# AdaLN attention and mixture-of-experts block: two-part modulation load, and another order of the prologue's products

## The reference

```python
mod = (silu(c) @ wmod).reshape(8, 6, 1, 128)
sa, ca, ga, sb, cb, gb = mod[:, 0], ..., mod[:, 5]   # gates ga, gb: size at least 0.25
h = layernorm(x) * (1 + ca) + sa
q, k, v = einsum('bsx,xAnh->Abnsh', h, w);  q = q + q_bias
a = q @ k.T * 64 ** -0.5 + relative_causal(q @ emb.T)
#   emb = sinusoids @ positional
x = x + ga * (softmax(masked(a)) @ v @ out_kernel + out_bias)
h = layernorm(x) * (1 + cb) + sb
x = x + gb * moe(h)        # 16 experts, capacity 256, one expert a token
```

## Time and profile before

| | us |
|---|---|
| median of 3 runs | 893.81 (893.18 to 894.71) |
| the profiled execution | 891.26 |
| its span, first to last instruction | 889.4 |
| PE busy / ACT busy / DVE busy in it | 865.1 / 710.7 / 667.8 |
| mean granted clock of PE | 0.992 |

### The profile page before, as it was taken

The page is one execution under the profiler, slowest core; times in us unless marked ns, Lnnn a source line. Parts: engine busy times, 40 slices in busy tenths (PEclk is TensorE's granted clock), DMA queues, the critical chain, the costliest instruction groups (busy, mean ns, idle before and its releaser), DMA issues.

```text
span 889.4 us, 17673 instructions
## 1 busy us (share of the span) xinstructions
PE 865.1 (97%) x5607; PEld 689.4 (78%) x5607; DVE 667.8 (75%) x2059; ACT 710.7 (80%) x1978; POOL 532.5 (60%) x796
## 2 busy tenths in 40 slices
PE   7999999999999999999999999999999999999994
PEld 6777777777777887777877777877777887777894
DVE  4778777786779677777879677877778677865794
ACT  4888889888888888888888889888888888873441
POOL 2655555666656765666566755676657646663454
PEclk8999999999999999999999999999999999999998
DMA  7000790000000100000000000000000000005960
GB/s 286 4 1 1 204 247 14 13 19 18 13 14 1 37 1 13 13 19 18 14 13 1 27 13 13 1 21 2 13 13 12 11 13 13 3 28 180 299 210 22
DMA packets 25053, 41.29 MB, mean 46 GB/s; under 512 B 3286, under 2 KB 17095, under 8 KB 24576
## 3 DMA queue, kind: packets, MB, share of 16 engines
q1 hardware_dynamic: 21600, 33.86, 12.7%
q0 software_dynamic: 3072, 5.94, 1.9%
q10 hardware_dynamic: 288, 0.36, 0.1%
HBM read 25.80 MB, written 16.82 MB: 48 GB/s over the span
## 4 chain that ended last, share of the span: by engine, by line
PE 82%; POOL 4%; issue 3%; DVE 1%; ACT 1%; DMA 1%; POOLq 0%; DVEq 0%; ACTq 0%
PE bank L858 22%; PE bank L823 16%; PE bank L888 16%; PE bank L868 15%; PE bank L895 5%; PE bank L844 4%; POOL out L510 3%; PE bank L855 3%; ACT prob L617 0%; POOL prob L455 0%; DMA x<-xbuf 0%; PE bank L903 0%; PE bank L808 0%; PE bank L1048 0%; PE bank L924 0%
## 5 line engine op out<-in xcount | busy, mean ns | idle before, releaser
L455 POOL TENSOR_SCALAR prob<-prob,rsum 128x128 f32<-128x128 f32 (+3 forms) x512 | 263.9, 534 | 221.8 <-DVE rsum L1233 216.1
L617 ACT ACTIVATE prob<-srow,nmax 128x512 f32<-128x512 f32 (+3 forms) x512 | 286.6, 561 | 65.7 <-DVE nmax L1221 62.5
L1221 DVE CUSTOM_DVE_ANT_0 srow<-bank,consts 128x512 f32<-128x512 f32 (+3 forms) x512 | 247.0, 488 | 88.2 <-issue 66.9
L868 PE MATMUL bank<-consts,prob 128*128 128x128 f32 x1280 | 201.9, 272 | 0.2 <-POOL prob L455 0.2
L868 PEld LDWEIGHTS bank<-consts,prob 128*128 128x128 f32 x1280 | 158.3, 141 | 22.7 <-issue 0.6
L448 POOL TENSOR_TENSOR qlo<-qx,qhi 128x384 fp32r<-128x384 f32 x128 | 129.1, 1009 | 49.5 <-ACT qhi L582 48.2
L626 ACT ACTIVATE pt<-bank 128x384 f32<-128x384 f32 x318 | 152.0, 495 | 1.4 <-PE bank L868 1.3
L888 PE MATMUL bank<-pt,v 128*64 128x512 f32 (+3 forms) x1024 | 152.0, 439 | 0.3 <-issue 0.2
L858 PE MATMUL bank<-khi,qhi 128*128 128x512 f32 (+2 forms) x384 | 145.7, 379 | 3.1 <-DVE nmax L1221 1.9
L1238 DVE SCALAR_TENSOR_TENSOR qx<-bank,qbias,consts 128x512 f32<-128x512 f32 x128 | 94.2, 736 | 60.2 <-PE bank L823 60.1
L858 PE MATMUL bank<-khi,qlo 128*128 128x512 f32 (+2 forms) x384 | 130.0, 339 | 0.0
(11 more groups left out here) (194 smaller groups left out, 1420.1 us busy)
## 6 DMA issues: line engine op xcount, KB each, us to landing
xbuf<-fill SPq DMA_DIRECT2D x4, 1540.0 KB, 23.2
x<-xbuf SPq DMA_DIRECT2D x14, 385.0 KB
raw<-in_w SPq DMA_DIRECT2D x16, 256.0 KB
prob<-in_w SPq DMA_DIRECT2D x16, 256.0 KB
h2T<-in_xt SPq DMA_DIRECT2D x8, 256.0 KB, 2.7
out<-row SPq DMA_DIRECT2D x8, 256.0 KB, 2.3
x<-in_x SPq DMA_DIRECT2D x1, 1792.0 KB, 13.3
modb<-mod_rows SPq DMA_DIRECT2D x1, 1536.0 KB, 7.3
```

The lines of the kernel that those rows point to most:

```text
L455: end = gp.tensor_scalar(part, part, rsum[:, par, 4 * h + q:4 * h + q + 1], 1.0, ALU.mult, ALU.mult)
L617: act.activation(prob[:, par, h, QOFF[q]:QOFF[q] + P * (q + 1)], srow[:, k % 4, 0:P * (q + 1)], ACT.Exp, bias=nmax[:, par, k:k + 1], scale ...
L868: last = pe.transpose(out[:, n * P:(n + 1) * P], prob[:, par, h, QOFF[q] + k * P:QOFF[q] + (k + 1) * P], ident)
L1221: dve.tensor_tensor_reduce(out=srow[:, k % 4, 0:w], in0=scb[k % 2][:, 0:w], in1=mask[:, S - w:S], scale=-1.0, scalar=BIG, op0=ALU.add, op1 ...
```

## The change

Six things are edited; the rest of the kernel is the same.

- `wmod` is loaded in two parts, sections 0 and 1 (128 KB) and 2 to 5 (256 KB), from ACT's queue behind its two loads, where it was one load on SP's queue, fifth there.
- Only the products of sections 0 and 1 stand ahead of the transposes. Those of 3, 4 and 2 follow them, into another PSUM bank, behind a wait for the second load.
- DVE copies the first two to `modT` ahead of `low_g(0, 1)`, and the three others behind `low(0)` (vlo). Later readers wait for `modT` 3, and TensorE too in round 2 of the first step, ahead of writing that bank.
- `w_table(1, 4)` moves from before the query products to behind the key product; `high_g` and `low_g` of pairs 1 to 3 move behind the key's evacuation on ACT and DVE.
- On ACT the cast of V's weights (`high_wv`) moves ahead of `high_q(0, 0)`.
- Fillers: 30 become 20, 16 become 8, the 8 behind `w_table(1, 4)` go, 16 become 6.

```diff
--- before.py
+++ after.py
@@ -258,7 +258,6 @@
             sp.dma_start(smallT[:, :], cols_d).then_inc(s["small"], 16)
             sp.dma_start(ident, consts_d[:, 0:128]).then_inc(s["ident"], 16)
             sp.dma_start(h2T[HD:P, :], ktab_d).then_inc(s["ktab"], 16)
-            sp.dma_start(wmod[:, :, :], wmod_d.rearrange("p (a b) -> p a b", a=6)).then_inc(s["wmod"], 16)
             sp.dma_start(consts[:, 512:], consts_d[:, 128:]).then_inc(s["consts"], 16)
             for h in range(2):
                 sp.dma_start(kx[HD:P, h, :], ktab_d[:, 0:P]).then_inc(s["kxt"], 16)
@@ -523,6 +522,9 @@
 
             act.dma_start(x[:, 2:QT, :], x_d[:, 2:QT, :]).then_inc(s["x0"], 16)
             act.dma_start(wall[:, 0:1, :], wall_d[:, 0:1, :]).then_inc(s["wall0"], 16)
+            wmod_v = wmod_d.rearrange("p (a b) -> p a b", a=6)
+            act.dma_start(wmod[:, 0:2, :], wmod_v[:, 0:2, :]).then_inc(s["wmod"], 16)
+            act.dma_start(wmod[:, 2:6, :], wmod_v[:, 2:6, :]).then_inc(s["wmodb"], 16)
 
             def high_g(a0, a1, after, name):
 
@@ -718,11 +720,11 @@
             high_wq(1, 4, 0)
             high_wq(1, 4, 1)
             high_wk(1, 4)
-            high_g(1, 4, 3, "whi")
+            high_wv()
             high_q(0, 0)
-            high_wv()
             evac_k(0, 0)
             evac_k(0, 1)
+            high_g(1, 4, 3, "whi")
             batches(turn)
             def high_w1(r, landed):
 
@@ -795,11 +797,15 @@
 
             pe.wait_ge(s["silu"], 1)
             pe.wait_ge(s["wmod"], 16)
-            for i, m in enumerate((0, 3, 1, 4, 2)):
-                last = pe.matmul(bank[0][:, i * B:(i + 1) * B], wmod[:, m, :], silu[:, 3, :], start=True, stop=True)
-            last.then_inc(s["mod_mm"], 1)
+            def mod_table(out, *sections):
+
+                for i, m in enumerate(sections):
+                    last = pe.matmul(out[:, i * B:(i + 1) * B], wmod[:, m, :], silu[:, 3, :], start=True, stop=True)
+                last.then_inc(s["mod_mm"], 1)
+
+            mod_table(bank[0], 0, 1)
             pe.wait_ge(s["ident"], 16)
-            idle(30)
+            idle(20)
 
             def turn_x(n, out=xtb):
 
@@ -809,9 +815,11 @@
                 last.then_inc(s["t_x"], 1)
 
             turn_x(0, opb)
+            pe.wait_ge(s["wmodb"], 16)
+            mod_table(trb[1], 3, 4, 2)
             pe.matmul(otb[0:B, 0:3 * D], silu[:, 3, :], wmod[:, 3:6, :].rearrange("p a d -> p (a d)"),
                       start=True, stop=True).then_inc(s["mod_mm"], 1)
-            idle(16)
+            idle(8)
 
             def project(out, a, cols, n, name):
 
@@ -956,6 +964,7 @@
             def first_step(k):
 
                 if k == 2:
+                    pe.wait_ge(s["modT"], 3)
                     w_table(4, PAIRS)
                 if k == 4:
                     pe.wait_ge(s["wv"], 2)
@@ -1028,18 +1037,17 @@
                         pe.wait_ge(s["wgc"], 2)
                     project_q(j + 1, n, m, 1, 8 * B if last and V_OF[a][0] else j + 4 if before else 2)
 
-            pe.wait_ge(s["wall1"], 16)
-            w_table(1, 4)
-            idle(8)
             pe.wait_ge(s["fhi"], 3)
             pe.wait_ge(s["flo"], 3)
             project_q(0, None, 0, 0)
             project_q(0, None, 0, 1)
             project_k(0, None, 0)
+            pe.wait_ge(s["wall1"], 16)
+            w_table(1, 4)
             pe.wait_ge(s["wall2"], 16)
             b_table(1, PAIRS)
             pe.wait_ge(s["hn"], 1)
-            idle(16, opb)
+            idle(6, opb)
             pe.wait_ge(s["kxt"], 32)
             pe.wait_ge(s["kt"], 4)
             def fill_in(n):
@@ -1195,13 +1203,10 @@
             dve.tensor_tensor(wlo[:, 0, 2 * P:3 * P], wall[:, 0, P:2 * P], whi[:, 0, 2 * P:3 * P], ALU.subtract)\
                 .then_inc(s["flo"], 1)
             xhat1(0)
+            dve.wait_ge(s["mod_mm"], 1)
+            dve.tensor_copy(modT[:, 0, :], bank[0][:, 0:B]).then_inc(s["modT"], 1)
+            dve.tensor_scalar(modT[:, 1, :], bank[0][:, B:2 * B], 1.0, None, ALU.add).then_inc(s["modT"], 1)
             low_g(0, 1, "fhi", 3, "flo")
-
-            dve.wait_ge(s["mod_mm"], 1)
-            half = lambda c: bank[0][:, c * B:(c + 2) * B].rearrange("p (i b) -> p i b", i=2)
-            dve.tensor_copy(modT[:, 0:3:2, :], half(0)).then_inc(s["modT"], 1)
-            link(dve.tensor_copy(modT[:, 4, :], bank[0][:, 4 * B:5 * B]))
-            dve.tensor_scalar(modT[:, 1:4:2, :], half(2), 1.0, None, ALU.add).then_inc(s["modT"], 1)
 
             def low_table():
 
@@ -1211,6 +1216,10 @@
 
             low_table()
             low(0)
+            dve.wait_ge(s["mod_mm"], 2)
+            link(dve.tensor_copy(modT[:, 2, :], trb[1][:, 0:B]))
+            link(dve.tensor_scalar(modT[:, 3, :], trb[1][:, B:2 * B], 1.0, None, ALU.add))
+            dve.tensor_copy(modT[:, 4, :], trb[1][:, 2 * B:3 * B]).then_inc(s["modT"], 1)
 
             def scores(j, par, k):
 
@@ -1362,7 +1371,7 @@
 
                 spread = lambda t: t.rearrange("p (b e) -> p b e", e=E)
                 if i == 0:
-                    dve.wait_ge(s["modT"], 2)
+                    dve.wait_ge(s["modT"], 3)
                     dve.memset(ones32, 1.0).then_inc(s["scr"], 1)
                     dve.memset(wgc[:, :, E:2 * E], 0.0).then_inc(s["scr"], 1)
                     for half, m in ((0, 3), (1, 2)):
@@ -1495,16 +1504,16 @@
             def rows_of():
 
                 dve.wait_ge(s["misc"], 48)
-                dve.wait_ge(s["mod_mm"], 2)
+                dve.wait_ge(s["mod_mm"], 3)
                 dve.tensor_copy(mrow[:, :, :].rearrange("p a d -> p (a d)"), otb[0:B, 0:3 * D]).then_inc(s["mev"], 1)
 
             dve.wait_ge(s["consts"], 16)
             dve.wait_ge(s["open"], 1)
             dve.wait_ge(s["bias"], 2)
-            low_g(1, 4, "whi", 4, "wlo")
             evac_q(0, 0, 0)
             evac_q(0, 0, 1)
             low_k(0, 0)
+            low_g(1, 4, "whi", 4, "wlo")
             batches(turn)
             def low_w1(e, par):
                 slot = e % 8
```

More of the change, by code:

```diff
@@ L185, in program @@
         mod_dram = nc.dram_tensor("mod_rows", [B, 3 * D], F32).ap()
-        names = ("ident consts open small wall0 wall1 wall2 w_v ktab kxt wlq x0 x1 wmod misc b2 wo zero "
+        names = ("ident consts open small wall0 wall1 wall2 w_v ktab kxt wlq x0 x1 wmod wmodb misc b2 wo zero "
                  "e_silu silu wg_mm bias xtl xtb bga scr csum wgc fhi flo whi wlo wlo_k mod_mm modT mev mrow modb gates "
```

## The result

| | kernel before | changed kernel |
|---|---|---|
| executions taken side by side | 893.49 us (4 executions, 892.18 to 894.71) | 885.49 us (4, 885.19 to 887.17) |
| ratio of the two, 95% interval | | 0.9919, 0.9906 to 0.9932 |
| all executions of the study | 893.55 us (78) | 885.93 us (14, 884.69 to 887.38) |
| profiled execution | 891.26 us | 885.63 us |
| first DVE operation on scores | 23.38 us | 18.66 us |

The two profiled executions differ by 5.6 us, of which 4.7 are there at the first scores.

A forecast was written before the change was run, and what follows sets the result against it. TensorE's matmul chain bounds the kernel, so only the first scores' start (22.29 us) can move. Transposes 5.0 us earlier plus 0.2 behind them give 5.2, taken from 893.81: 888.6 us, range 887.7 to 891.4.

The forecast's parts named there:

- The place and the mechanism: Prologue: xn is complete at 8.79 us but transposes start at 13.96, behind the weights' wait, products and fillers; 5.2 us gained.
- 4.35 to 7.5: Bounds in us for the landing of the load of sections 0 and 1 on ScalarE's queue; 6.2 was taken.
- The table load: On ScalarE, delayed by two more issues from 1.65 to 2.6 to 2.8 us; costs 0 to 0.1, 0.1 taken.
- xn as the floor of the transposes: Prologue: products and fillers end between 8.0 and 9.2 us, xn is there at 8.89, so transposes start at about 9.0.
- my two prices for fillers: Ahead of the transposes: 20 fillers cost 1.3 us at 0.067 each or 2.1 us at 0.105.
- whatever starts earlier there should end earlier by as much: From the first scores matmul (22.29 us before) to the end, everything moves rigidly if nothing behind is tied to a fixed time.
- the moved evacuations: high_g and low_g behind the key's evacuation end at 17.5 and 18.1 us, just before scores want DVE at 18.2; cost nothing.
- its distance of 2.55 us to the median: Whole kernel: the median lies 2.55 us above the profiled 891.26, so the 5.2 were taken from 893.81.
- The clock rival: Prologue: TensorE's clock falls to 1.2 GHz while the projections run; gain only 2.1 to 2.8 us, 891.0 to 891.7; chance 0.18.
- The second rival: Prologue: the new loads save only time of issue, landing at 7.5; gain 3.8 to 4.5 us, 889.3 to 890.0; chance 0.13.
- The slower case: The clock falls and stays down into attention's first steps; slower by 0.2% if down until 27 us; chance 0.04.
- given back: Scores start 5 us earlier, but wall2 or the first batch's loads come late and steps wait: 893 to 894; chance 0.07.

The follow-up runs named there:

- h_before_short: The kernel before with 4 fillers instead of 30 ahead of the transposes, nothing else: 889.26 us, ratio 0.9957.
- all four delayed versions: The changed kernel with 18, 42 - 6, 54 or 90 more fillers directly ahead of the first scores (1, 2, 3, 5 us): 889.45, 890.89, 889.11, 891.57 us.
- j_stats_tail: The changed kernel with DVE's statistics ahead of silu, fillers 20 to 6 and 8 to 4, and 30 fillers at the wait for expert 2's rows: 886.88 us.
- e3_bridge: The kernel before with 30 more fillers in TensorE's idle stretch ahead of the wait for the modulation weights: 888.85 us, ratio 0.9955.
- f2_tail_before: The kernel before with 30 fillers where TensorE waits for the rows of expert 2, near the end: 891.79 us, ratio 0.9987.
- e1_loads: The kernel before with only the modulation weights' load split in two on ScalarE's queue: 891.63 us, ratio 0.9986.
- e4_fillers: The changed kernel with 30, 16 and 16 fillers, as before, instead of 20, 8 and 6: 889.04 us.
- h_delay1: The changed kernel with 18 more fillers directly ahead of the first scores, a delay of 1 us: 889.45 us.
- j_again: The changed kernel without an edit, run and profiled again: median 885.99 us.

## Why the prediction was wrong

**Right, in size too.**
- The place and the mechanism: TensorE waited for the weights, then ran products and fillers, while xn lay ready. In the four executions of the unedited kernel before the first scores on DVE are at 23.36 to 23.93 us, in the three of the changed one at 18.24 to 18.66: 5.1 us between the medians, and 5.2 were forecast. First scores on PE 17.15, 17.27 and 17.57, forecast 17.1.
- The load landed at 5.05, inside 4.35 to 7.5; taking 6.2 was harmless, since TensorE was not free before 6.0 to 6.4.
- The table load started 1.0 us later, as worked out, and silu 0.13 us later; 0.1 was forecast. In the other executions, of all versions, silu waits longer for the small parameters and starts anywhere between 4.2 and 5.2 us; xn follows it.
- DVE's, ScalarE's and SyncE's waits cost nothing; wall2 had landed 1.9 us ahead of its use.

**Small errors that cancel.** TensorE was taken as free from 5.5 and xn as the floor of the transposes. In the first profiled execution the first fillers ran at 1.2 GHz to the end, so the products began at 6.37 and the 20 fillers held the transposes to 9.33 instead of 9.0; the upper of my two prices for fillers (0.105) was the right one there. In the two others xn was the floor, and came later (transposes at 9.32 and 9.45), behind a silu at 4.46 and 4.60.

**What failed is the step from the first scores to the end**: "whatever starts earlier there should end earlier by as much". Two terms, and both gain:
- *Attention is 0.85 us shorter.* It takes 771.2 to 771.3 us in seven of the eight profiled executions with the old order (771.0 in h_before_short) and 770.2 to 770.5 in all twelve with the new. I had called the moved evacuations zero, and they nearly are: at the entry of step 1 TensorE waits less for POOL's qlo (0.57 us before, 0.25 now), but 0.2 of this is lost again within the step, to a longer wait for DVE. Some 0.7 us are two pauses of DVE, ahead of its first operation on scores of step 4 and of step 31. Before:

```profile
72.44 0.69 DVE L1221 CUSTOM_DVE_ANT_0 srow<-bank,consts 128x512 f32<-128x512 f32 x1 [0.40 <-issue]
```

```profile
400.03 0.69 DVE L1221 CUSTOM_DVE_ANT_0 srow<-bank,consts 128x512 f32<-128x512 f32 x1 [0.39 <-issue]
```

After:

```profile
67.27 0.69 DVE L1230 CUSTOM_DVE_ANT_0 srow<-bank,consts 128x512 f32<-128x512 f32 x1
```

```profile
394.43 0.69 DVE L1230 CUSTOM_DVE_ANT_0 srow<-bank,consts 128x512 f32<-128x512 f32 x1
```

Behind each of the two, 3.7 us later, TensorE pauses too, for 0.34 us, ahead of scores (at 76.12 and 403.71). All eight profiled executions with the old order have both pauses (0.39 to 0.41 us), and the twelve with the new order have neither (0.03 to 0.05). So they go with the program, not with chance; what DVE waits for there the profile does not show ("issue"), and the cause stays open.

- *The end is shorter*, by 1.1 us in the medians of the profiled executions (97.5 to 96.4); the medians of all executions leave 1.7 for it. Four executions against three, which overlap (94.8 to 97.7 and 94.9 to 96.7), don't prove this term; it is what is left when the two others are taken away.

5.1 + 0.85 + 1.1 = 7.05, beside 7.6 measured. The second term is also why the base was wrong: 891.26 was a lucky execution of the kernel before, and I carried its distance of 2.55 us to the median over to a kernel that doesn't have it: the profiled execution of the changed kernel lies 0.3 us from its median. With one profiled execution and three times above it, that distance should have been read as something that the profile does not show, which a change may take away; the range had room for it to grow less, and none for it to grow more.

**The rivals.** The clock rival occurs (all four delayed versions, j_stats_tail), but in none of the three profiled executions of the changed kernel, and where it occurs it costs 1.5 to 2 us, not 2.4 to 3.1. That the clock could also *give* something was missing: e3_bridge shows that the idle stretch by itself, closed, was worth 4.7 us, 2.6 at the first scores. The second rival, a landing at 7.5, and with it the strict reading of the Trainium skill ("DMA: Bandwidth & Descriptors", section "Issuing engines are not separate DMA queues"), did not happen: 128 KB came 3.4 us after the issue, and even the second part, behind it, landed at 2.14 + 5.1 = 7.2. No run here separates the place in the row of loads from the time of issue, so the page's rule is not shown wrong; only what I made of it was. (The smaller gain of this rival adds up to 3.7 us, not 3.8.) The slower case and "given back" did not occur.

**Open.** What ended the two pauses in attention. Why the last scatter ends 0.8 to 1.7 us later in three of five profiled executions with the prologue before (f2_tail_before counted), in e1_loads and e4_fillers, in two of the four delayed ones, and in none of the changed kernel's three. A step at a certain moment does not fit the delays; chance alone would give medians that rise with the delay, and 3 us of it took less than 2. Why the clock fell in all four delayed prologues and in none of the four undelayed ones that run the same program up to there. The moment at which the clock first rises differs between executions of one kernel too (5.41, 5.48 and 10.28 us in the changed one); what sets it no run here shows.

## What to carry to other kernels

Profile the kernel before several times when a change of half a per cent is at stake, and cut each execution at the same few marks: a distance between the profile and the median is a cost that the profile doesn't show, and belongs to a stage. An idle stretch of TensorE in a prologue can cost more than itself: in the kernel before, what followed it ran at half the clock for almost 6 us. Ask first whether work can be moved into it, then what cheap filler there would bring, and take fillers out of places where data already waits. Don't take "it starts x earlier" for "it ends x earlier" without a look at the waits at the far end, and compare the middle too, step by step: a reordered program can gain or lose short pauses far from the edit.

## What the runs showed of the hardware

- A filler of 128 columns takes 0.107 us at 1.2 GHz and 0.056 at 2.4 (from start to start), a modulation product's instruction 0.22 and 0.12. With such a ruler the clock can be read where the profile has no record of it: in the changed kernel's first profile its 1.00 was wrong up to 10.28 us.
- Fillers at full clock end sooner and leave idle time, and the clock can fall about such a wait: 1.39 us of waiting with a fall at 9.11 in h_delay1. It need not: 1.58 us of waiting without a fall in j_again.
- DVE paused for 0.4 us where the profile shows nothing that it waited for, at the same two operations in all eight executions with the old order, and at neither in the twelve with the new.
- The end of an indirect scatter, as SyncE sees it, varies by 1.4 us between executions of the same kernel (27.7 to 29.1 us after the last scores, with the issue at 25.3 in the two looked at).
